# Indirect writes of a routed layer in two bursts, and its first loads ahead of the inverse copies

## The chip, the cores and the metric

The kernel runs on one core of a Trainium2 chip. The metric is the device time of one execution in microseconds. Engines are TensorE (PE), VectorE (DVE), ScalarE (ACT), GpSimd (POOL) and the DMA queues that SyncE, ScalarE and GpSimd feed.

## The reference, cut to what matters

Four layers work on x (8 sequences of 256 rows, 256 columns) and on a context of the same shape, all in float32, each adding to x:

```
x = x + mlstm_attention(layernorm(x), ctx, ctx)             # layer 1
x = x + moe32(layernorm(x))                                 # layer 2
x = x + fft_convolution_and_two_ffns(ctx, layernorm(x))     # layer 3
x = x + dense_moe8(x)                                       # layer 4

# layer 2, moe32: 2048 tokens, top 4 of 32 experts, H = 128
weights, indices = top_k(softmax(xf @ Wg), 4)
for e in range(32):
    tok = tokens that chose e (at most 1024)
    y[tok] += (silu(xf[tok] @ W1[e]) * (xf[tok] @ W3[e])) @ W2[e] * weight
out = y + silu(xf @ Ws1) * (xf @ Ws3) @ Ws2                 # shared expert

# layer 3, the part computed beside layer 2: a long convolution of the context
zn = layernorm(ctx @ W_in + b_in) * g + beta
dcw = irfft(rfft(filter) * rfft(zn))                        # first rows, per sequence
```

## The kernel before, in words

All engines run their own instruction streams and meet in semaphores. After the attention the stretch that matters has four strands, which overlap.

**Shared expert and context rows.** TensorE computes the shared expert of layer 2 in eight steps; VectorE multiplies (line 663), rounds (the cast of line 668) and forms the low part (line 810, `hL`) of each step, since every float32 product is made of a high and a low part. Between these steps VectorE takes statistics of the context rows `zn`, ScalarE normalises them (line 1325, semaphore `z_normed`), and gain and shift are put on: for quarters 0 and 1 by VectorE (lines 803 and 804, behind steps 6 and 7), for quarters 2 and 3 by POOL (`affine(2)` and `affine(3)`, lines 1660 and 1661, two passes over 128 x 1024 each).

**Routing writes on POOL.** Each of the 2048 tokens goes into four slots of a buffer in HBM, `slots_in`, ordered by expert. POOL does it with 64 indirect writes (`scatter`, line 1642), each of one row per partition, 128 rows of 1 KB, whose places come from `idS`. All signal one semaphore, `scattered`, and behind every fourth POOL waits until all writes so far have landed. The order on POOL is written out by hand: 32 writes, affine(2), 8 writes, affine(3), 24 writes, then `split_expert(e)` for the 32 experts: two passes over 128 x 768 each (line 1633 copies the high part of the weights from stage `eS` into the ring `eHL` of six, line 1635 makes the low part). In front of expert 3 POOL waits for the last product of the transform (`prod_dve` 6) and the last spectrum, because the ring slots of experts 3 to 5 lie on the buffers of the spectra. Experts 0 to 2 have no such wait.

**The transform.** It goes in six blocks, n = 0 to 5. TensorE makes a spectrum (line 1969), ScalarE copies it (line 1336, `Zs`), VectorE multiplies it with the filter's spectrum in seven instructions (lines 836, 837, 839 to 843), each waiting for the one before, and TensorE transforms back (line 1985). Line 839 must wait for the inverse of the block before, since it overwrites `PR`; lines 836 and 837 need not. `PI`, written by line 843, releases the inverse. The order on TensorE is spectrum 0, spectrum 1, then spectrum n + 2 and inverse n in turns; in front of the last inverse stand 32 spare matmuls (line 1719), which compute nothing that is used. Blocks 2 and 5 work on two quarters of the rows each. ScalarE copies the results out of PSUM into `dcw` (`inverse_copy`, line 1330): copies 0 and 1 between spectrum copies, copies 2 and 3 behind the last inverse.

**The routed tiles.** 48 pairs of tiles of 128 slots. ScalarE gives out the loads (`load_pair`, line 1361, a ring of four) and rounds; TensorE transposes a pair (line 2008), waiting at first for all eight inverse copies (`inv_copied` 8), multiplies it with its expert's weights (`tile_up`, line 2028, waiting for `ew_ready`), transposes and multiplies again (lines 2037 and 2047); VectorE forms low parts (line 850). The stores go to `slots_out`, from which POOL later gathers (line 1687). After them come the feed-forward blocks of layer 3 and the 32 expert blocks of layer 4 (lines 1921 and 1937).

## Time and profile before

| | us |
|---|---|
| median of 3 runs | 1806.13 (1804.2 to 1808.56) |
| span of the profiled execution | 1787.3 |
| median less that span | 18.8 |
| TensorE busy | 1667.1 (93%) |
| VectorE busy | 1207.9 (68%) |
| ScalarE busy | 474.6 (27%) |
| POOL busy | 471.5 (26%) |
| mean granted TensorE clock, share of full | 0.971 |

The span runs from the first to the last instruction of one execution; the device time of that same execution is not listed apart from the three runs, so it stands beside their median. Times below count from the span's start. In a timeline a row is: start, duration, engine, line, operation, written and read tensors, and in brackets the idle time before it and what ended it. ACTq is ScalarE's issuing of DMAs. TensorE's full clock is 2.4 GHz, its lower level 1.2 GHz (0.50). The writes of line 1648 lie between 213.3 and 350.8, the transform between 268 and 349, the routed tiles between 354 and 513.

### The profile page before, as it was taken

How to read it: one execution, taken by the hardware profiler on the slowest of the kernel's cores; microseconds unless marked ns; L12 is line 12 of the kernel's file. 1: busy time of each engine (PE TensorE's matmuls, PEld its weight loads, DVE VectorE, ACT ScalarE, POOL GpSimd, SP SyncE). 2: the span in 40 equal slices, each digit the busy share in tenths (PEclk: the TensorE clock that was granted, in tenths of full speed). 3: DMA queues.
4: the chain of work that ended last, by engine and by line, in shares of the span. 5: the costliest groups of instructions: out<-in, count | busy, mean ns of one | idle time of the engine just before them, and what ended most of it. 6: DMA issues, size and time to landing. Idle time of an engine off the chain costs nothing.

```text
span 1787.3 us, 29133 instructions
## 1 busy us (share of the span) xinstructions
PE 1667.1 (93%) x9784; PEld 1439.4 (81%) x9785; DVE 1207.9 (68%) x2483; ACT 474.6 (27%) x836; POOL 471.5 (26%) x355
## 2 busy tenths in 40 slices
PE   6998987799956898999999999999999999999998
PEld 5997673388854787888888888888888888888887
DVE  6457777556656895666666766766766766766765
ACT  3445322134432464211211211211111111111111
POOL 4274257688426601100100100100100100100100
PEclk9998999899978998999999999999999999999999
DMA  9200022278643200000000000000000000000001
GB/s 368 91 1 30 16 73 96 89 250 272 200 127 119 72 1 19 19 36 18 19 34 18 20 33 18 21 32 18 21 32 18 23 30 18 26 27 18 18 0 48
DMA packets 53827, 106.53 MB, mean 60 GB/s; under 512 B 6528, under 2 KB 37696, under 8 KB 53632
## 3 DMA queue, kind: packets, MB, share of 16 engines
q1 hardware_dynamic: 19920, 63.33, 10.4%
q10 hardware_dynamic: 27696, 25.51, 4.5%
q0 software_dynamic: 6144, 16.79, 2.9%
q8 instruction: 43, 0.70, 0.2%
q14 instruction: 24, 0.20, 0.0%
HBM read 69.96 MB, written 35.65 MB: 59 GB/s over the span
## 4 chain that ended last, share of the span: by engine, by line
PE 80%; DVE 6%; issue 4%; POOL 4%; DMA 4%; ACT 2%; SPq 0%; POOLq 0%; DVEq 0%; another core or an unknown queue 0%; ACTq 0%
PE ps L1921 39%; PE ps L1937 20%; PE ps L2028 4%; DMA slots_in<-xn,idS 2%; POOL slots_in L1648 2%; PE ps L2047 2%; PE ps L1772 2%; PE ps L2103 1%; PE ps L2125 1%; PE ps L2008 1%; DVE x L917 1%; DMA x<-in_x 1%; PE ps L1773 1%; PE ps L1789 1%; PE ps L1790 1%
## 5 line engine op out<-in xcount | busy, mean ns | idle before, releaser
L1921 PE MATMUL ps<-xTH,wH 128*128 128x512 f32 x1024 | 402.5, 393 | 2.1 <-DVE hF L1161 2.1
L1921 PE MATMUL ps<-xTH,wL 128*128 128x512 f32 x1024 | 402.2, 393 | 0.0
L1921 PE MATMUL ps<-xTL,wH 128*128 128x512 f32 x1024 | 398.9, 390 | 0.0
L1309 ACT ACTIVATE sg<-ps 128x512 f32<-128x512 f32 x264 | 157.9, 599 | 885.3 <-PE ps L1921 885.3
L1161 DVE TENSOR_TENSOR hF<-sg,ps 128x512 f32<-128x512 f32 x256 | 175.7, 686 | 302.1 <-ACT sg L1309 302.1
L1620 POOL TENSOR_TENSOR wL<-wS,wH 128x1536 fp32r<-128x1536 f32 x32 | 111.9, 3496 | 959.8 <-ACT wH L1304 959.8
L1937 PE MATMUL ps<-wL,hH 128*128 128x256 f32 x1024 | 289.8, 283 | 0.0
L1937 PE MATMUL ps<-wH,hL 128*128 128x256 f32 x1024 | 289.7, 283 | 0.0
L1937 PE MATMUL ps<-wH,hH 128*128 128x256 f32 x1024 | 288.6, 282 | 0.5 <-DVE hL L1170 0.5
L1170 DVE TENSOR_TENSOR hL<-hF,hH 128x512 fp32r<-128x512 f32 x256 | 258.0, 1008 | 0.1
L1921 PEld LDWEIGHTS ps<-xTL,wH 128*128 128x128 f32 x1024 | 192.8, 188 | 42.2
L1180 DVE SCALAR_TENSOR_TENSOR x<-ps,cw,x 128x256 f32<-128x256 f32 x512 | 222.6, 476 | 1.0 <-PE ps L1937 1.0
L1921 PEld LDWEIGHTS ps<-xTH,wH 128*128 128x128 f32 x1024 | 193.6, 189 | 36.1 <-ACT sg L1309 1.9
L1921 PEld LDWEIGHTS ps<-xTH,wL 128*128 128x128 f32 x1024 | 193.8, 189 | 30.5
L1937 PEld LDWEIGHTS ps<-wH,hH 128*128 128x128 f32 x1024 | 195.5, 191 | 10.6 <-DVE hL L1170 0.7
L1937 PEld LDWEIGHTS ps<-wH,hL 128*128 128x128 f32 x1024 | 195.5, 191 | 9.8
L1937 PEld LDWEIGHTS ps<-wL,hH 128*128 128x128 f32 x1024 | 195.5, 191 | 0.0
L1164 DVE CAST hH<-hF 128x512 fp32r<-128x512 f32 x256 | 109.3, 427 | 38.8 <-PE ps L1937 30.2
L1648 POOL DMA_INDIRECT slots_in<-xn,idS x64 | 76.6, 1197 | 59.6 <-DMA slots_in<-xn,idS 29.7
L2028 PE MATMUL ps<-eHL,hH 128*128 x384 | 81.5, 295 | 2.2 <-POOL eHL L1635 2.2
L1687 POOL DMA_INDIRECT yg<-slots_out,idG x48 | 50.0, 1041 | 69.2 <-DMA slots_out<-yo 49.0
L603 DVE SCALAR_TENSOR_TENSOR Cm<-ps,Dm 128x384 f32<-128x384 f32 x64 | 35.6, 557 | 47.1 <-ACT Dm L1272 43.0
(385 smaller groups left out, 2525.4 us busy)
## 6 DMA issues: line engine op xcount, KB each, us to landing
wS<-in_w SPq DMA_DIRECT2D x32, 768.0 KB, 4.3
slots_in<-eS SPq DMA_DIRECT2D x16, 768.0 KB, 20.2
eS<-in_wr SPq DMA_DIRECT2D x32, 384.0 KB, 3.9
xl<-slots_in ACTq DMA_DIRECT2D x48, 256.0 KB, 3.9
slots_out<-yo ACTq DMA_DIRECT2D x48, 256.0 KB, 3.1
cx<-in_ctx SPq DMA_DIRECT2D x1, 2048.0 KB, 10.4
x<-in_x SPq DMA_DIRECT2D x2, 1024.0 KB, 13.8
out<-x SPq DMA_DIRECT2D x4, 512.0 KB, 2.9
```

Of the source, the lines that this page charges most:

```text
L1161: dve.tensor_tensor(hF[:, b, :], sg[:, b, :], ps[:, 2 + b, :], ALU.mult).then_inc(mul_done, 1)
L1164: dve.tensor_copy(hH[:, b, :], hF[:, b, :]).then_inc(h_high, 1)
L1170: dve.tensor_tensor(hL[:, b, :], hF[:, b, :], f32(hH[:, b, :]), ALU.subtract).then_inc(h_low, 1)
L1180: dve.scalar_tensor_tensor(x[:, tile, :], acc, cw2[:, tile, bass.ds(it, 1)], x[:, tile, :], ALU.mult, ALU.add).then_inc(evac_done, 1)
L1309: act.activation(sg[:, b, :], ps[:, b, :], ACT.Silu).then_inc(silu_done, 1)
L1620: pool.tensor_tensor(blocks(wL, slot, plain), blocks(wS, slot, plain), f32(blocks(wH, slot, plain)), ALU.subtract).then_inc(w_low, 1)
L1648: pool.indirect_dma_start(xs_d, bass.IndirectOffsetOnAxis(ap=idS[:, n, k:k + 1], axis=0), xn[:, n, :], None, bounds_check=TILES * P - 1, o ...
L1687: pool.indirect_dma_start(slot_rows(n)[:, k, :], None, ys_d, bass.IndirectOffsetOnAxis(ap=idG[:, n, k:k + 1], axis=0), bounds_check=TILES ...
L1772: pe.matmul(ps[:, i % 2, 0:256], kT[:, c, t0:t0 + P], qM[:, i % 12, :], start=True, stop=True)
L1921: last = pe.matmul(ps[:, 2 * half + b, :], piece(w, s, slot, col, P), v[:, k, g * 512:(g + 1) * 512], start=q == 0, stop=q == 5)
L1937: last = pe.matmul(o, h[:, b, t * P:(t + 1) * P], piece(w, s, slot, col, D), start=(opens and t % 2 == 0 and q == 0), stop=(closes and q = ...
L2028: last = pe.matmul(ps[:, 2 + b, t * D:(t + 1) * D], h[:, b, (2 * t + k) * P:(2 * t + k + 1) * P], eFlat[:, bass.ds(off + (w + k * D), D)], ...
```

## The change

Three edits:

- POOL's writes signal two semaphores in turns, one burst of four on the one, the next on the other. Behind each burst from the second on POOL waits for the landing of the burst before, no longer for its own. Behind the last write it waits for the last burst.
- ScalarE waits for both semaphores in place of the one.
- On ScalarE that wait, three more that stood with it, and the first four `load_pair` are moved in front of `inverse_copy(2)`, `inverse_copy(3)` and the wait for the last product.

```diff
-        scattered = sem("scattered")
+        scattered = [sem("scattered_even"), sem("scattered_odd")]
@@ scalar
             spectrum_copy(5)
-            inverse_copy(2)
-            inverse_copy(3)
-            act.wait_ge(prod_dve, 6)
...
-            act.wait_ge(scattered, 64 * 16)
+            for burst in scattered:
+                act.wait_ge(burst, 64 * 8)
             act.wait_ge(evac_done, 4 * M_FA)
             wait_low(act, 8)
             act.wait_ge(table_done, 1)
             for q in range(4):
                 load_pair(q, q)
+            inverse_copy(2)
+            inverse_copy(3)
+            act.wait_ge(prod_dve, 6)
             for q in range(2):
                 tile_high(q, q)
                 load_pair(q + 4, q)
@@ gpsimd, scatter
-                                            bounds_check=TILES * P - 1, oob_is_err=False).then_inc(scattered, 16)
+                                            bounds_check=TILES * P - 1, oob_is_err=False).then_inc(scattered[sent[0] // 4 % 2], 16)
                     sent[0] += 1
-                    if sent[0] % 4 == 0:
-                        pool.wait_ge(scattered, 16 * sent[0])
+                    if sent[0] % 4 == 0 and sent[0] > 4:
+                        before = sent[0] // 4 - 2
+                        pool.wait_ge(scattered[before % 2], 64 * (before // 2 + 1))
@@ gpsimd
             scatter(NT * TOPK - 40)
+            pool.wait_ge(scattered[1], 64 * 8)
             pool.wait_ge(table_done, 1)
```

## Rows read from the trace of the kernel before

**Rows 1.** The page's chain that ended last, by line.

```profile
PE ps L1921 39%; PE ps L1937 20%; PE ps L2028 4%; DMA slots_in<-xn,idS 2%; POOL slots_in L1648 2%; PE ps L2047 2%; PE ps L1772 2%; PE ps L2103 1%; PE ps L2125 1%; PE ps L2008 1%; DVE x L917 1%; DMA x<-in_x 1%; PE ps L1773 1%; PE ps L1789 1%; PE ps L1790 1%
```

**Rows 2.** The chain of waits, 340 to 380: start, us, what.

```profile
358.04 2.92 PE ps L2028 x12
363.62 1.43 PE ps L2028 x12
```

**Rows 3.** POOL's timeline, 348 to 358: start, us, instruction, idle before.

```profile
348.38 0.97 POOL L1648 DMA_INDIRECT slots_in<-xn,idS  x1 [0.30 <-issue]
350.88 1.46 POOL L1633 TENSOR_TENSOR eHL<-eS,zcol 128x768 fp32r<-128x768 f32 x1 [1.52 <-DMA slots_in<-xn,idS]
355.72 1.81 POOL L1635 TENSOR_TENSOR eHL<-eS,eHL 128x768 fp32r<-128x768 f32 x1
```

**Rows 4.** Timelines of ScalarE, TensorE and VectorE, 349 to 357.

```profile
349.03 2.06 ACT L1330 ACTIVATE dcw<-ps 128x512 f32<-128x512 f32 x4 [24.12 <-PE ps L1985]
350.87 1.96 ACTq L1361 DMA_DIRECT2D xl<-slots_in  x4
353.87 1.94 PE L2008 MATMUL ps<-ident,xl 128*128 128x128 f32 x8 [4.88 <-DMA xl<-slots_in]
355.69 1.48 DVE L850 TENSOR_TENSOR hL<-ps,hH 128x512 fp32r<-128x512 f32 x2 [12.28 <-ACT hH L1370]
```

**Rows 5.** Line 1648: durations min/median/max in ns, and POOL's idle time before it.

```profile
L1648 POOL DMA_INDIRECT slots_in<-xn,idS x64: 967/976/3037, 213.3 to 348.4; - x64
  DMA slots_in<-xn,idS: 29.7, 13
```

**Rows 6.** Timelines around the shared experts: ScalarE, VectorE and TensorE, 253 to 266.

```profile
253.53 2.07 ACT L1325 ACTIVATE zn<-zn,sd,rs 128x256 f32<-128x256 f32 x4
259.08 0.69 DVE L810 TENSOR_TENSOR hL<-hF,hH 128x512 fp32r<-128x512 f32 x1
265.33 0.51 PE L1937 MATMUL ps<-sH,hH 128*128 128x256 f32 x1 [2.62 <-DVE hL L810]
```

**Rows 7.** POOL's groups, 299.9 to 350.5: busy, mean ns, idle before.

```profile
L1648 POOL DMA_INDIRECT slots_in<-xn,idS x24 | 32.8, 1366 | 17.4 <-DMA slots_in<-xn,idS 11.2 <-issue 5.5 <-POOL zn L1661 0.8
```

**Rows 8.** Timelines of POOL and VectorE where both compute, 274 to 300.

```profile
293.51 2.35 POOL L1660 TENSOR_TENSOR zn<-zn,bcv 128x1024 f32<-128x1024 f32 x1 [1.52 <-DMA slots_in<-xn,idS]
295.94 3.20 POOL L1661 TENSOR_TENSOR zn<-zn,bcv 128x1024 f32<-128x1024 f32 x1
274.04 4.35 DVE L836 TENSOR_TENSOR tv<-Zs,WG 128x2048 f32<-128x2048 f32 x1 [4.39 <-ACT Zs L1336]
293.70 3.25 DVE L842 TENSOR_TENSOR tv<-tv 128x1024 f32<-128x1024 f32 x1
296.98 2.71 DVE L843 TENSOR_TENSOR PI<-tv 128x512 f32<-128x512 f32 x1
```

**Rows 9.** Timelines of VectorE and POOL, 310 to 314.

```profile
310.45 2.29 DVE L836 TENSOR_TENSOR tv<-Zs,WG 128x2048 f32<-128x2048 f32 x1
310.77 2.81 POOL L1648 DMA_INDIRECT slots_in<-xn,idS  x1 [0.30 <-issue]
```

**Rows 10.** VectorE's timeline, end of the first product.

```profile
284.18 0.69 DVE L843 TENSOR_TENSOR PI<-tv 128x512 f32<-128x512 f32 x1
```

**Rows 11.** VectorE's groups, 271.3 to 350.

```profile
L840 DVE TENSOR_TENSOR tv<-Zs,WG 128x1024 f32<-128x1024 f32 x6 | 7.4, 1226 | 0.2
L839 DVE TENSOR_TENSOR PR<-tv 128x512 f32<-128x512 f32 x6 | 4.2, 692 | 10.3 <-PE ps L1985 10.3
```

**Rows 12.** Line 1985 by stretch: window, length, busy (x), granted clock, DMA, GB/s.

```profile
286.70:290.30 3.60, 3.55 (x8) 1.33 (x7) 1.00 0.20 72
299.70:305.00 5.30, 5.25 (x8) 2.08 (x8) 0.69 0.10 36
331.70:338.10 6.40, 6.33 (x8) 2.41 (x8) 0.58 0.13 44
```

**Rows 13.** POOL's timeline after sixteen gathers.

```profile
545.21 1.12 POOL L1687 DMA_INDIRECT ya<-slots_out,idG  x1 [4.80 <-DMA yg<-slots_out,idG]
```

## The prediction

> **What bounds the kernel now.** I read the page's chain first: TensorE's matmuls carry it, and lines 1921 and 1937 alone, the experts of the last layer, are 59% [rows 1]. The change touches none of that. It touches the 75 us ahead of the routed tiles, where the chain runs over POOL's indirect writes. I therefore read the end of that stretch. The first product of the tiles (line 2028) starts at 358.04 [rows 2]. Two branches lead to it. On POOL the last write is issued at 348.38, its landing is awaited, and four passes of 1.46 to 1.82 us split experts 0 and 1 by 357.53 [rows 3]. On the other side the inverse transform ends on TensorE at 349.0, ScalarE makes four copies, only then gives out the first pair loads at 350.87, and TensorE waits 4.88 us for the data until 353.87; VectorE has the first low part at 355.69 + 0.74 = 356.4 [rows 4]. POOL is the last of the two, by 1.1 us (the product starts 0.5 us behind its release), and the loads are right behind. I call the end of the inverse transform X: X = 349.0, and the tiles start at X + 9.05.
>
> **The bursts.** POOL waits 29.7 us in 13 places for a landing [rows 5]. With two bursts out, the older burst has 4 x 1.28 us to land, against 2.5 us from the last issue to its landing (348.38 to 350.88), so I take every such wait as gone; an issue gap of 0.30 stays: 29.7 - 3.9 = 25.8 us. The first 32 writes then take 32 x 1.28 = 41 us from 213.3 and, I allow, 1.5 more for collisions: the first affine on POOL starts at about 256, 15 us sooner (seven waits of 2.0 net, and a landing of 1.5), just when its input is ready (253.53 + 2.07) [rows 6]. Its two passes take 4.7, then 8 writes some 12.5 with their collisions: the second affine starts near 273.5 in place of 293.5. The 24 writes left had a mean of 1.37 us [rows 7] and a gap of 0.30: 40 us from 279, the end near 319, and with the landing the first expert pass near 320 in place of 350.9.
>
> **What that sets free, and what it collides with.** POOL is then no longer the last branch. But experts 0 to 2 are not held back by the products (only expert 3 is), so their six passes, 3 x (1.47 + 1.82) = 9.9 us, move from behind the products into them. The trace says what two such instructions do to each other. POOL's pass at 293.51 ended at 295.86; VectorE's pass begun at 293.70 took 3.25 us, and ended 1.1 us after POOL's; POOL's next pass then took 3.20 against the first one's 2.35, and VectorE's next one 2.71. The first product's multiply at 274.04 took 4.35, too [rows 8]. Undisturbed, such passes of VectorE take 2.29, 0.69 and 1.23 us [rows 9 to 11]. Each waits for the other's end, in turns. In the same way an indirect write begun at 310.77 ended 0.84 us after the multiply begun at 310.45. The Trainium skill (SBUF — State Buffer, Who interferes with whom) states that a VectorE instruction with two SBUF inputs and a GpSimd one that reads SBUF exclude each other, the second waiting in full. That speaks against this change, and the rows agree; the sum below goes by the rows.
>
> Step by step, against X:
>
> 1. The first affine moves to 256 to 261, into the shared experts. VectorE's low part at 259.08 has two SBUF inputs and will wait for POOL's second pass. VectorE sets the end of this stage: TensorE waits for its last low part until 265.33 [rows 6]. I take +2.0 us. Bounds: 0 if it fits between, and 4.7 if both passes lie on VectorE's way. The cast of line 668 has one input, and no row shows it beside a POOL pass, so I leave it at nothing. By the skill's same section a cast may take the shared ports as well; by that the step would be nearer its upper end.
> 2. The second affine lands on the first product, in place of the first affine there (+2.06 before, about the same now). That product has cover: its last multiply ended at 284.87 and the first inverse, behind a spectrum on TensorE, began only at 286.7 [rows 10, 12]. Cost 0; if both passes hit, 2.3 more against 1.9 of cover, so up to 0.4.
> 3. The second product loses its collision: -(3.25 - 1.23) - (2.71 - 0.69) = -4.05 us. TensorE then idles 4 us less before the second inverse. That inverse ran at a granted clock of 0.69, half speed for part of it, and took 5.3 us; the first one, right behind a spectrum, ran at 1.00 and took 3.6 [rows 12]. I take -1.65, with 0 as the other end.
> 4. The six expert passes start near 320, in the fifth product. The products run in a ring: the inverse on TensorE, then lines 839 to 843 on VectorE (0.69 + 3 x 1.23 + 0.69, 5.2 with gaps) [rows 11], then the next inverse. Lines 836 and 837 of the next product lie beside the inverse, with a mean slack of 10.3 / 5 = 2.1 us before line 839. So one or two passes hide there and four or five alternate with lines 839 to 843, each costing its length less 0.13. I went through it with the first pass at 320, 322, 324 and 328 and got 6.5, 5.5, 5.3 and 6.0. I take +6.2. Ends: 0 if these passes do not hold VectorE, and 9.9 if all of them are on its way.
> 5. The fifth inverse already starts cold (0.58, 6.4 us) [rows 12]. Before it TensorE will now idle 6 us longer; I keep its price, with 6.4 x 0.58 / 0.50 = 7.4, so +1.0, as the upper end. The 32 spare matmuls still lie under the last product.
>
> X moves by 2.0 - 4.05 - 1.65 + 6.2 = +2.5, to 351.5.
>
> 6. Behind X: ahead of the copies ScalarE is idle for 24 us, from the last spectrum copy on [rows 4]; the writes have landed near 320, so the four loads' 1.96 us of issue falls into that idle time, and the data are there long before X. The wait on the writes stands in front of two inverse copies, whose input comes 30 us after the writes; it holds nothing. TensorE then transposes right behind the copies: X + 2.2 in place of X + 4.9. From there to the first product the old path took 356.4 - 353.87 = 2.6 us. X + 4.8 in place of X + 9.05, with experts 0 and 1 long split: -4.25. Experts 3 to 5 may start with the last product, 5 us ahead of X, so no tile waits for them. The first 12 matmuls of the tiles ran in 2.92 us, later ones in 1.43 [rows 2]; if the shorter idle time keeps the clock up, another -1.5. I take -0.3 of it.
>
> Sum: +2.5 - 4.25 - 0.3 = -2.0 us. The tiles are a chain on TensorE, and all behind them is dependent, so this passes to the end. The profiled execution's span is 1787.3 us; the runs' median is 1806.1, so 18.8 us lie around the span, and I leave them as they are: 1804.1 us. About 0.2% (3.6 us) is what a measurement of this kernel can tell from no change.
>
> **Rivals.**
> A, the collisions cost little. Only affine passes of 1024 columns are seen to hold a product; beside the expert passes VectorE so far ran instructions with a PSUM input alone. If step 4 is 0 to 1, the sum is -2.0 - 5.7 = -7.7: 1798.4. Against it: line 1635 reads two tensors just as the affine does. 0.27.
> B, slower: POOL keeps the ports from one pass to the next. Its passes follow one another within 0.08 us; it gave way to VectorE in the one pair that I can see [rows 8]. If it does not in this place, step 4 costs 9.9 (+3.7), the fifth inverse stays cold throughout (+1.0) and steps 1 and 2 go to their ends (+2.7 + 0.4): -2.0 + 7.8 = +5.8, 1811.9. It decides from 5.6 us above my sum. 0.12.
> C, the writes pile up, so POOL is done no sooner. For: after bursts of 16 indirect gathers POOL waited 4.80 us for the last landing, not 1.5 [rows 13]. Against: those gathers were themselves issued without a stall. The loads would then still be issued before the copies, and 2 us of issue would be given back: -1 to +1, 1806. 0.09.
>
> **The numbers.** My forecast has 0.52: 1804.1, its own range 1800.5 to 1807.5 (steps 1, 3 and 6 at their nearer ends); 0.06 of it reaches below -3.6 us and 0.01 above +3.6. Faster: 0.27 + 0.06 = 0.33. Slower: 0.12 + 0.01 = 0.13. Same: 0.54. The range 1797.5 to 1808.5 takes in A and leaves out most of B.
>
> **What would show it.** Right: no wait of POOL for a landing between bursts; the last write issued near 318; experts 0 to 2 split between 320 and 335, and in that stretch four or five of VectorE's multiplies at 2.3 to 3 us; lines 842 and 843 of the second product back at 1.23 and 0.69; inverse end near 351.5; the first tile product about 5 us behind it. Wrong: multiplies of 1.23 beside the expert passes and X near 345 (A); expert passes back to back with a multiply of 4 us or more beside them (B); writes of more than 2 us with no multiply beside them (C).

## The result, and the profile after

The change made the kernel slower: 1830.9 us (median of 5, 1829.7 to 1838.3) against 1804.2 us (1799.1 to 1808.6) on the same chip, a ratio of 1.0169 (95% interval 1.0145 to 1.0192). That is 27 us between the medians and 30 us by the ratio. The forecast was 1804.1 with a range of 1797.5 to 1808.5.

POOL did what was foreseen. The first and the last of the first 32 writes, then the first pass of the first affine (POOL's timeline of the changed kernel):

```profile
211.51 1.39 POOL L1649 DMA_INDIRECT slots_in<-xn,idS  x1 [13.63 <-issue]
...
251.92 0.97 POOL L1649 DMA_INDIRECT slots_in<-xn,idS  x1 [0.30 <-issue]
277.08 2.39 POOL L1662 TENSOR_TENSOR zn<-zn,bcv 128x1024 f32<-128x1024 f32 x1 [24.19 <-ACT zn L1325]
```

Between 211.51 and 251.92 the writes follow one another at 1.28 us, without a wait. But where POOL was to go on at 256, as `z_normed` was signalled at 255.6 before [rows 6], it waits 24.19 us for it, until 277.08. The reason lies in the other engines, in the same 40 us. VectorE and ScalarE (timelines of the changed kernel):

```profile
253.66 0.34 DVE L763 COPY etf<-ps 1x192 f32<-1x192 f32 x1 [27.33 <-remote]
...
257.45 0.60 ACT L1309 ACTIVATE sg<-ps 128x512 f32<-128x512 f32 x1 [27.14 <-remote]
```

TensorE (timeline, 228 to 260):

```profile
228.40 0.49 PE L1952 MATMUL ps<-ident,tc 96*1 96x96 f32 x4
...
231.04 0.40 PE L1924 MATMUL ps<-xTH,sH 128*128 128x512 f32 x1
231.27 0.40 PE L1924 MATMUL ps<-xTH,sL 128*128 128x512 f32 x1
...
232.55 0.40 PE L1924 MATMUL ps<-xTH,sH 128*128 128x512 f32 x1 [0.22 <-issue]
233.96 0.39 PE L1924 MATMUL ps<-xTH,sL 128*128 128x512 f32 x1 [1.01 <-issue]
234.68 0.48 PE L1924 MATMUL ps<-xTM,sH 128*128 128x512 f32 x1 [0.34 <-issue]
236.09 0.40 PE L1924 MATMUL ps<-xTH,sH 128*128 128x512 f32 x1 [0.94 <-issue]
...
258.59 0.58 PE L1940 MATMUL ps<-sH,hH 128*128 128x256 f32 x1 [19.88 <-DVE hL L810]
```

VectorE's line 763 needs only the small transposes of 228.40, over at 228.9. It starts at 253.66, 25 us later; ScalarE's line 1309 needs a product that TensorE had done at 238.7 and starts at 257.45, 19 us later. "remote" is the name for a wait whose end no recorded signal explains. Both end behind the last write (251.92 + 0.97). In the kernel before, the same line 763 started 0.04 us behind the end of its transposes (230.71):

```profile
230.75 0.35 DVE L763 COPY etf<-ps 1x192 f32<-1x192 f32 x1 [2.60 <-PE ps L1949]
```

TensorE slows down as well before it stops: from 232.55 on its matmuls start 1.41, 0.72 and 1.41 us apart instead of 0.23 (231.04 to 231.27), with idle time put down to "issue". So three engines stand still while POOL's writes stream: VectorE and ScalarE for 27 us, TensorE for 20, the last of it waiting for VectorE. The windows say the same. Columns: stretch, length, busy time and instructions of PE, PEld, DVE, ACT and POOL, clock, DMA share, GB/s. The changed kernel:

```profile
213.00:253.00 40.00, 21.33 (x91) 14.28 (x91) 9.45 (x27) 4.87 (x7) 30.55 (x31) 0.80 0.28 102
```

The same stretch of the kernel before:

```profile
213.00:253.00 40.00, 36.34 (x173) 28.10 (x174) 31.54 (x104) 10.69 (x19) 23.18 (x23) 0.96 0.20 72
```

VectorE is busy for 9.45 us instead of 31.54, TensorE for 21.33 instead of 36.34. The DMA engines are busy 0.28 of the time, so they are not full. And in the changed kernel's chain of waits (start, us, what) the piece is this:

```profile
226.32 27.31 another core or an unknown queue
```

The expert passes then hit the transform, as foreseen, though in the fourth product and not in the fifth (changed kernel, POOL, then VectorE):

```profile
340.25 1.46 POOL L1634 TENSOR_TENSOR eHL<-eS,zcol 128x768 fp32r<-128x768 f32 x1 [1.59 <-issue]
341.79 2.13 POOL L1636 TENSOR_TENSOR eHL<-eS,eHL 128x768 fp32r<-128x768 f32 x1
343.88 2.45 POOL L1634 TENSOR_TENSOR eHL<-eS,zcol 128x768 fp32r<-128x768 f32 x1
...
329.62 1.22 DVE L842 TENSOR_TENSOR tv<-tv 128x1024 f32<-128x1024 f32 x1
...
340.63 1.63 DVE L839 TENSOR_TENSOR PR<-tv 128x512 f32<-128x512 f32 x1 [5.40 <-PE ps L1988]
342.29 2.71 DVE L840 TENSOR_TENSOR tv<-Zs,WG 128x1024 f32<-128x1024 f32 x1
345.03 2.37 DVE L841 TENSOR_TENSOR tv<-Zs,WG 128x1024 f32<-128x1024 f32 x1
347.44 2.71 DVE L842 TENSOR_TENSOR tv<-tv 128x1024 f32<-128x1024 f32 x1
350.18 1.84 DVE L843 TENSOR_TENSOR PI<-tv 128x512 f32<-128x512 f32 x1
```

One more loss lies just ahead of that product, and no step of the prediction has it: the wait of 5.40 us of line 839, against 2.03 in the kernel before. The third inverse took 8.9 us (331.6 to 340.5, granted clock 0.62) where before it took 5.5 (310.4 to 315.9, granted clock 1.00). TensorE had idled 1.9 us ahead of it in both, so what brought the clock down is not shown. Four of its matmuls, changed kernel and kernel before:

```profile
334.34 2.08 PE L1988 MATMUL ps<-PR,GI 64*128 64x512 f32 x4
...
312.22 1.13 PE L1985 MATMUL ps<-PR,GI 64*128 64x512 f32 x4
```

And the end of the transform, the loads and the first tile (ScalarE, TensorE, VectorE; answers to [rows 2, 4]):

```profile
352.29 1.96 ACTq L1358 DMA_DIRECT2D xl<-slots_in  x4
379.33 2.06 ACT L1330 ACTIVATE dcw<-ps 128x512 f32<-128x512 f32 x4 [25.34 <-PE ps L1988]
...
381.50 1.06 PE L2011 MATMUL ps<-ident,xl 128*128 128x128 f32 x8 [2.20 <-issue]
384.83 0.58 PE L2031 MATMUL ps<-eHL,hH 128*128 x1 [2.27 <-DVE hL L850]
...
382.92 1.29 DVE L850 TENSOR_TENSOR hL<-ps,hH 128x512 fp32r<-128x512 f32 x2 [9.20 <-ACT hH L1367]
```

The loads are given out at 352.29, 27 us ahead of the copies; X is 379.3 and the tiles start at X + 5.5, where before it was X + 9.05 [rows 2, 4].

Executions reach this stretch at different times, so from here on I measure from one mark that stands ahead of all that changes: the start of TensorE's last `ps<-ident,tc` transposes (228.40 after, 230.22 before, 227.5 to 236.1 in the other kernels). From the mark to the first tile's product it is 127.8 us before and 156.4 us after, +28.6. The input of POOL's first affine comes 23 us later (48.5 against 25.4), and the first product ends 24.9 us later. The second inverse then comes another 3.8 us later (the spectrum ahead of it took 8.80 us against 7.1). The second product, free of its collision, gives 4.1 back and its inverse 1.5. The third inverse adds 3.4, the expert passes 6.2, the rest is -0.5, and the path behind X gives 3.55 back. That is the 30 us of the ratio, to within what a measurement tells. A single profile tells such sums to some 3 us only: two other kernels (of the gathers, below) have the code of the kernel before up to the tiles, and there it is 130.5 and 127.7 us. The two profiled spans differ by more, 46.1 us, for two reasons that have nothing to do with the change: the profiled execution after took 1835.2 us for a span of 1833.4, so only 1.8 us lie around a span, and that of before was therefore a 1789 us one, below all of its timed runs; and among the gathers the changed kernel's has waits "remote" that before's has not (below).

### The profile page after: what moved, and what is told of

Its sections match the earlier page's. It is cut to its first block, busy times and chain, and to the rows that moved or that the text cites. A ratio compares the mean times of both kernels' runs of the same rounds, so it can differ in the third digit from the quotient of the medians.

```text
span 1833.4 us, 29134 instructions
## 1 busy us (share of the span) xinstructions
PE 1678.4 (92%) x9784; PEld 1446.4 (79%) x9785; DVE 1213.8 (66%) x2483; ACT 474.7 (26%) x836; POOL 470.7 (26%) x355
## 4 chain that ended last, share of the span: by engine, by line
PE 81%; DVE 9%; issue 4%; ACT 2%; another core or an unknown queue 2%; DMA 1%; SPq 0%; DVEq 0%; ACTq 0%
PE ps L1924 39%; PE ps L1940 20%; PE ps L2031 4%; PE ps L2050 2%; PE ps L1775 2%; PE ps L1988 2%; PE ps L2106 1%; PE ps L2128 1%; PE ps L2011 1%; PE ps L1972 1%; DMA x<-in_x 1%; DVE x L917 1%; PE ps L1776 1%; PE ps L1792 1%
## 5 line engine op out<-in xcount | busy, mean ns | idle before, releaser
L1649 POOL DMA_INDIRECT slots_in<-xn,idS x64 | 73.1, 1142 | 33.8 <-issue 29.2
```

The source lines that it names most:

```text
L1649: pool.indirect_dma_start(xs_d, bass.IndirectOffsetOnAxis(ap=idS[:, n, k:k + 1], axis=0), xn[:, n, :], None, bounds_check=TILES * P - 1, o ...
```

## The experiments

The name "the standstill" is used for the waits above. Theory S: a stream of indirect writes without a gap causes it, and it is the whole loss. Rivals: L, the hoisted loads do it; K, the collisions with the expert passes.

**The bursts alone, and the loads alone.** The first has the new waits of POOL with ScalarE's order of before; the second has ScalarE's new order with the waits of before.

> The two bursts alone; the loads stay behind the last inverse copies. Theory S (stream): 32 indirect writes given out by POOL with no pause for 41 us hold back the signals that TensorE sends, so VectorE stands still for some 27 us until the last of them is out. Then this kernel has the same standstill (VectorE line 763 starts within 1 us of the end of the 32 writes, 25 to 28 us late) and the whole loss: 1828 to 1835 us. Rival L (the hoisted loads or the wait in front of the copies cause the loss): 1800 to 1806 and no standstill. Rival K (collisions of VectorE's multiplies with POOL's passes of experts 0 to 2 cause it): 1806 to 1812, no standstill, multiplies of 2.3 us and more.

> The hoisted loads alone, on the kernel before; one burst in flight. Theory S: no standstill, and POOL is still the last branch at the first tile, so 0 to +2 us against the kernel before: the four loads' 2 us of issue now lies in front of the last copies when the writes land only at 350.8. Rival L: 20 us or more slower. Rival K: as S.

The bursts alone gave 1827.8 against 1800.9, ratio 1.0157 (1.0133 to 1.0180); the loads alone 1801.8, ratio 1.0004 (0.9990 to 1.0018). L falls. S was met in the time and for ScalarE, but only in part for VectorE. Its line 763 was expected 25 to 28 us late, at the end of the writes; it started at 243.16, 12.7 us late and 11 us ahead of that end. The bursts alone have the standstill all the same (waits of that kernel, 210 to 300: who, for what, sum, times, longest):

```profile
ACT sg L1309 <- remote: 29.2, 1, 29.2
...
DVE etf L763 <- remote: 15.2, 1, 15.2
```

The loads alone gain nothing for a reason of their own: without the bursts the writes land near 351, ScalarE waits for them in front of inverse copies 2 and 3, and the copies come at 353.43, though the inverse was over at 345.8. The tiles start 130.8 us behind the mark. ScalarE's timeline of the loads-alone kernel:

```profile
351.44 1.95 ACTq L1358 DMA_DIRECT2D xl<-slots_in  x4
353.43 2.06 ACT L1330 ACTIVATE dcw<-ps 128x512 f32<-128x512 f32 x4 [30.75 <-issue]
```

**A gap after every fourth write.** The changed kernel with linked memsets of one column; eight of them, then two:

```diff
+                    if sent[0] % 4 == 0:
+                        for _ in range(8):      # in the second kernel: 2
+                            link(pool.memset(zcol[:, :], 0.0))
```

> The changed kernel, and POOL sets one column of zeros eight times, in a chain, behind every fourth write: a pause of about 2 us that waits for no landing. Theory S: the stream has holes again, the standstill of VectorE at line 763 is gone or under 3 us, and the time is 1798 to 1808. Rival F (what matters is how many writes are in flight, not the lack of a pause): by the time of the pause all but the last write have landed in both, so this rival can only say that the landing wait itself matters: standstill kept, 1825 to 1835. Rival K: 1806 to 1812.

> The changed kernel with two linked memsets of one column (about 0.3 us of work, a gap of some 1.2 us between writes instead of 0.30) after every fourth write; eight of them gave a gap of about 2.4 us and no standstill. At a landing of about 2.4 us after the issue, with a gap of 1.2 us the queue of writes is never empty. Theory P (a gap on POOL is what lets the others' signals through, however short): no wait 'remote' over 2 us, VectorE's L763 starts before 235, time 1800 to 1806. Rival Q (the queue of writes must run empty once): the standstill is there as in the changed kernel, L763 starts after 250, time 1820 to 1832. In between: a standstill of part of the length.

No standstill in either. Ratios 1.0006 (0.9987 to 1.0025) and 1.0026 (1.0008 to 1.0044): the loss of 1.7% is gone or nearly so. The second needs only this (its timeline, POOL and then VectorE):

```profile
229.72 0.28 POOL L1657 MEMSET zcol<- 128x1 f32 x2
230.80 0.97 POOL L1649 DMA_INDIRECT slots_in<-xn,idS  x1 [0.80 <-POOL zcol L1657]
...
229.66 0.35 DVE L763 COPY etf<-ps 1x192 f32<-1x192 f32 x1 [2.60 <-PE ps L1955]
```

The write before the memsets ended at 229.73, so the gap is 1.07 us. At 2.4 us from issue to landing, the median of this kernel's writes, the queue doesn't run empty in it, so that is not the condition. The kernel with eight memsets ran on the chip of the bursts alone, which has the standstill; that of two ran on another, but its gap in the first 32 writes was enough too on a chip where longer pieces have the standstill ("The best of both", below). S stands.

**Pacing the first 32 writes, with and without the collisions.** In the first of these kernels POOL waits for a burst's own landing in the first 32 writes and is two bursts deep behind them. The second also moves the wait for the sixth product in front of expert 0, so that all expert passes come behind the products. The third is the second with the four loads back behind the copies.

```diff
-                        before = sent[0] // 4 - 2
+                        before = sent[0] // 4 - (1 if sent[0] <= 32 else 2)
...
-                if e == 3:
+                if e == 0:
                     pool.wait_ge(prod_dve, 6)
```

> The changed kernel, but for the first 32 writes POOL waits for each burst's own landing as before; two bursts are in flight only in the last 32. Theory S: the long gapless stretch is gone from the shared experts; the later stretches of 8 and 24 writes lie beside the transform, where TensorE's signals are needed at every product. If any gapless stretch stalls, there is a standstill of up to 25 us there; in the changed kernel's trace none is seen beside the 24 writes, so I expect none: 1796 to 1806. Rival K: the expert passes collide with the multiplies as in the changed kernel (8 to 9 us in one product): 1806 to 1812.

> The version with the first 32 writes in paced bursts (wait for a burst's own landing) and the last 32 two bursts deep, with all of POOL's expert passes held until the sixth product is done (the wait for prod_dve stands before expert 0, not before expert 3). Theory K (the six expert passes and VectorE's products of 339 to 354 us hold each other up): the products L836 to L843 take 1.2 to 1.6 us again, L843 of the sixth ends about 350 in place of 356.7, the first tile's product starts near 366 in place of 372, and the time comes down from 1810 to about 1803. Rival C (TensorE's inverses at the low clock are what ends last there, the collisions are hidden beside them): L843 of the sixth ends within 2 us of 356.7 and the time stays at 1808 to 1812. Rival E (the experts are then late for the first expert tiles): the products are early but the first expert tile waits for POOL's L1636, time 1808 or more.

> The version with paced first bursts and late experts, but with the four pair loads back behind the last copies of the inverse transform, as in the kernel before. Step 6 of the prediction (with POOL done early, hoisting the loads takes 4.25 us off the way from the last copy to the first tile): the first tile's product starts 3 to 5 us later than in the run with the hoist (357.1 there, with 1788.4 us span) and the ratio to before is 0.002 higher than with it (0.999). Rival (the loads' landing is hidden behind the transposes' own work): the first tile's product within 1 us of it, the same ratio.

First: ratio 1.0050 (1.0029 to 1.0070), no standstill, 139.1 us from the mark to the tiles. Second: 0.9990 (0.9974 to 1.0005), 128.6 us. The passes beside the products thus cost some 10.5 us, as the ratios say too (0.6%). The first five instructions of the last product, with the passes beside them (VectorE, first kernel):

```profile
341.27 3.70 DVE L836 TENSOR_TENSOR tv<-Zs,WG 128x2048 f32<-128x2048 f32 x1
345.01 2.37 DVE L837 TENSOR_TENSOR tv<-tv 128x1024 f32<-128x1024 f32 x1
347.81 1.79 DVE L839 TENSOR_TENSOR PR<-tv 128x512 f32<-128x512 f32 x1 [0.43 <-PE ps L1988]
349.63 2.37 DVE L840 TENSOR_TENSOR tv<-Zs,WG 128x1024 f32<-128x1024 f32 x1
352.03 2.71 DVE L841 TENSOR_TENSOR tv<-Zs,WG 128x1024 f32<-128x1024 f32 x1
```

And without them (second kernel):

```profile
335.28 2.29 DVE L836 TENSOR_TENSOR tv<-Zs,WG 128x2048 f32<-128x2048 f32 x1
337.61 1.22 DVE L837 TENSOR_TENSOR tv<-tv 128x1024 f32<-128x1024 f32 x1
340.74 0.69 DVE L839 TENSOR_TENSOR PR<-tv 128x512 f32<-128x512 f32 x1 [1.90 <-PE ps L1988]
341.46 1.22 DVE L840 TENSOR_TENSOR tv<-Zs,WG 128x1024 f32<-128x1024 f32 x1
342.72 1.22 DVE L841 TENSOR_TENSOR tv<-Zs,WG 128x1024 f32<-128x1024 f32 x1
```

The five take 12.94 us with the passes beside them and 6.64 without, 6.3 less. The rest comes behind them: the last inverse took 9.0 us (356.7 to 365.7) after the slow products and 5.6 (345.9 to 351.5) after the quick ones. Its matmuls ran at half pace in most of it (2.08 us for four, against 1.13). K is true and worth 10 us, give or take the 3 us by which single profiles differ. The second kernel is as fast as the one before, no faster than it can be told. Third: ratio 1.0001 (0.9981 to 1.0021). From the first inverse copy to the first tile it takes 7.33 us (347.58 to 354.91) against 5.50 (351.55 to 357.05) with the loads hoisted. So with POOL early hoisting is worth 1.8 us here, half of what its expectation said, and less than a ratio can show. In the other kernels with the loads hoisted that path takes 5.5 us in some and 6.4 in others, so it is 1 to 1.9 us.

**How long may the stream be.** Four kernels change only where the first 32 writes are interrupted: a wait for the own landing behind writes 8, 16, 24 and 32; a gap of 1.1 us (two memsets) behind write 16 alone; behind write 24 alone; behind 8, 16 and 24.

```diff
-                        before = sent[0] // 4 - 2
+                        before = sent[0] // 4 - (1 if sent[0] in (8, 16, 24, 32) else 2)
```

```diff
+                    if sent[0] in (8, 16, 24):    # or == 16, or == 24
+                        for _ in range(2):
+                            link(pool.memset(zcol[:, :], 0.0))
```

> The changed kernel, but after writes 8, 16, 24 and 32 POOL waits until the burst it has just sent has landed (after the others one burst stays in flight). So the writes stream without a pause for 8 x 1.28 = 10.2 us and stand still for about 2.5 us. Theory S1 (signals are held only while the stream runs and get through at every pause): VectorE's L763 waits at most 10 us instead of 27, each hand-over between engines there loses up to one stretch of 10 us, and the time lies at 1803 to 1815. Rival S2 (it takes more than 10 us of unbroken stream before anything is held): no wait 'remote' over 2 us in 210 to 260 us, time 1799 to 1806. Rival S3 (what matters is the number of writes in flight at all, not the pauses): the 27 us standstill as before, 1828 to 1832.

> The changed kernel with one pause only (two linked memsets, a gap of 1.10 us) after write 16 of the first 32, so two unbroken stretches of 16 writes, 20 us each. In the changed kernel the other engines stopped about 18 us into the stretch (VectorE's L763 due at 230). Theory O (it takes a stretch of some 18 us before signals are held, and any gap starts the count again): the second stretch ends just before its hold would bite, no wait 'remote' over 3 us, time 1.000 to 1.003 of before. Rival A (a signal that is sent anywhere in an unbroken stretch is held to its end): waits 'remote' up to 20 us that end at the pause (near 232) and at the end of the second stretch (near 253), ratio 1.008 to 1.015.

> The changed kernel with one pause only, after write 24 (near 242 us), so an unbroken stretch of 24 writes, 31 us, and one of 8. Theory (the standstill ends with the unbroken stretch, whatever the other engines do meanwhile): VectorE's L763, due at 230, starts at 242 to 244 instead of 253.7, the wait 'remote' there is 13 to 16 us instead of 27.3, and the ratio to before is 1.006 to 1.012 instead of 1.017. Rival (the standstill lasts until all of the writes are through, or until a refill of instructions that comes at 259 in the changed kernel): L763 at 253 or later, ratio 1.015 to 1.019.

> The changed kernel with a gap of 1.1 us after writes 8, 16 and 24. Theory B (TensorE's signals are served more slowly than they are sent while the writes stream, a backlog builds up, and a gap serves a part of it; one gap was too little, seven were enough): with three gaps the waits 'remote' are between those, VectorE's L763 (due at 230) starts between 231 and 239 and ScalarE's L1309 waits 3 to 20 us instead of 27 to 29; ratio 1.003 to 1.012. Rival H (signals are held until the unbroken stretch ends): then each gap frees what was sent before it, nothing waits 'remote' for more than 10 us, ratio 1.002 to 1.005. Rival T (what counts is that a stretch stays under some 10 writes): no wait 'remote' over 2 us, ratio 1.001 to 1.003.

| interruption of the first 32 | median of before on that chip | longest unbroken | VectorE's wait at 763 | ScalarE's at 1309 | mark to tiles | ratio (interval) |
|---|---|---|---|---|---|---|
| none (the change) | 1804.2 | 32 | 27.3 | 27.1 | 156.4 | 1.0169 (1.0145 to 1.0192) |
| none, loads not hoisted | 1800.9 | 32 | 15.2 | 29.2 | 156.6 | 1.0157 (1.0133 to 1.0180) |
| gap after 24 | 1801.4 | 24 | 13.8 | 29.1 | 153.0 | 1.0136 (1.0100 to 1.0171) |
| gap after 16 | 1801.4 | 16 | 9.6 | 29.1 | 152.6 | 1.0125 (1.0094 to 1.0156) |
| gap after 8, 16, 24 | 1792.2 | 8 | 2.3 | 6.2 | 132.3 | 1.0000 (0.9984 to 1.0017) |
| landing after 8, 16, 24, 32 | 1792.7 | 8 | 2.4 | 6.2 | 134.9 | 1.0035 (1.0014 to 1.0056) |
| gap after each 4, in all 64 | 1792.7 | 4 | 2.6 | 6.2 | 136.1 | 1.0026 (1.0008 to 1.0044) |
| gap of 2.0 us after each 4, in all 64 | 1800.9 | 4 | 2.6 | 6.2 | 135.9 | 1.0006 (0.9987 to 1.0025) |
| landing after each 4 | 1800.9 | 4 | 2.6 | 6.2 | 139.1 | 1.0050 (1.0029 to 1.0070) |
| gap after each 4, experts late (below) | 1801.4 | 4 | 2.6 | 6.2 | 125.7 | 0.9990 (0.9970 to 1.0010) |
| kernel before: landing after each 4 | 1804.2 | 4 | 2.6 | 6.2 | 127.8 | 1 |

(About 2.6 and 6.2 us are what these two instructions wait in the kernel before, too.) Two more expectations fell. One gap behind write 16 was to cure all or to end the waits in front of it, and did neither. With the gap behind 24, line 763 should have started at 242 to 244; it started at 239.59, 2.6 us ahead of the gap, so a gap is not what lets it go, and the ratio was outside what was expected. ScalarE's wait was 29.1 us in both, to 3.4 us behind the last write. The kernel with the gap behind 24 (timeline; POOL, VectorE, ScalarE):

```profile
242.20 0.28 POOL L1657 MEMSET zcol<- 128x1 f32 x2
...
252.21 0.97 POOL L1649 DMA_INDIRECT slots_in<-xn,idS  x1 [0.31 <-issue]
...
239.59 0.34 DVE L763 COPY etf<-ps 1x192 f32<-1x192 f32 x1 [13.78 <-remote]
...
256.63 0.60 ACT L1309 ACTIVATE sg<-ps 128x512 f32<-128x512 f32 x1 [29.12 <-remote]
```

So signals are not simply held until a stream ends. They come late: there line 763's signal (its transposes ended at 228.4) came 11 us late, ScalarE's (its product ended at 233.0) 24 us. With three gaps nothing comes late at all, which rival T alone had said; with the landings of 8, S2 had.

What is shown: 16, 24 or 32 writes in one piece did harm, and 4 in one piece, with a gap or a landing behind them, did none on the same chips (medians of before of 1800.9 and 1801.4 us). The two rows with pieces of 8 prove less than they seem to. They were taken on the two other chips (1792.2 and 1792.7), where no profile of any kernel has a wait "remote", not even beside gathers that go out 16 in a piece, and where neither the change nor pieces of 16 or 24 writes ever ran. So that 8 writes (10 us) in one piece do no harm, as T and S2 have it, is not shown: it may have been the chip. A backlog that builds up in a long stretch and goes off in a gap when it is small fits the rows; that it was too large to go off in the one gap is argued, not shown.

**The gathers.** Behind the routed tiles POOL gathers in pieces of 16. The kernel before with a wait for the landing every 8 gathers, and with the 1.1 us gap (two memsets) behind every 4:

```diff
-                if n in (4, 8, 12):
+                if n in (2, 4, 6, 8, 10, 12, 14):
                     pool.wait_ge(gathered[(n - 1) % YG], ((n - 1) // YG + 1) * TOPK * 16)
```

> The kernel before, with POOL waiting for the landing of its gathers after every 8 (n = 2, 4, 6 ...) instead of after every 16. Theory G (the gathers' stream of 16 without a pause, too, makes the other engines stand still in some executions, and this is the 15 us by which the profiled execution of before lies under its median): each of the four added waits costs POOL about 2.5 us, 10 us in all, of which part is hidden, but no wait 'remote' over 2 us is left in 560 to 660 us and the runs lie closer together; time 1790 to 1800. Rival N (the gathers' stand-still is not of this kind, or doesn't reach the end): the four waits only add, 1801 to 1812.

> The kernel before, with two linked memsets (a gap of 1.1 us) after every fourth gather; the gathers otherwise run in unbroken stretches of 16, 20 us. Theory G (in some executions the gathers' stretches hold TensorE's signals up as the writes' do, waits 'remote' of 7 to 13 us near 610 to 650, and this is most of the spread of the runs of before; the waits for landings of the earlier run cost what they saved): the 16 gaps cost at most 0.8 us each on POOL, 12.8 us, partly beside the waits for VectorE; no wait 'remote' over 2 us in 540 to 660, a spread of the runs under 8 us and a ratio of 0.996 to 1.000. Rival N (the spread is of another kind): the same spread as before and a ratio of 1.000 to 1.006.

The reason for these was a row such as this, of the loads-alone kernel (waits, 540 to 720):

```profile
ACT xTH L1431 <- remote: 8.7, 2, 7.9
```

Ratios 1.0018 (1.0004 to 1.0032) and 1.0026 (1.0013 to 1.0040): the interruptions only cost, 3 and 5 us. But they were no test. Waits "remote" of 6 to 13 us among the gathers stand in all eight profiles taken on two of the chips, whose medians of before were 1800.9 and 1801.4 us, and in none of the eight taken on two others, at 1792.7 and 1792.2 us, whatever the kernel. These two kernels ran where there was nothing to remove. The profile of before doesn't fit a rule by chips, though: it has no such wait, at 1789 us against a median of 1804. What decides it stays open.

**The best of both.** The gap of 1.1 us after each fourth of the first 32 writes, all expert passes behind the products, loads hoisted; then the same with the gap every 4 and every 8 gathers. Its edits are those shown, with `sent[0] % 4 == 0 and sent[0] <= 32` for the gap.

> The changed kernel with two linked memsets after each fourth of the first 32 writes (the gap of 1.10 us that was enough), none after that, and POOL's expert passes held until the sixth product is done. If the two losses found (the standstill; the expert passes beside the products) are all there is against the change, the sixth product ends near 341 us on a chip where it ended at 349.8 with the passes beside it, the first tile's product starts at 352 to 354 against 358 to 359 in the kernel before, and the ratio to before is 0.995 to 0.998. Rival: TensorE's inverses at the low clock set the products' pace whatever POOL does; then the sixth product ends at 345 or later, the first tile's product is no earlier than 357 and the ratio is 0.999 to 1.001.

> The version with gaps in the first 32 writes and late experts (0.999 so far, its first tile's product 2.1 us earlier than in the kernel before, but with a wait 'remote' of 13.4 us among the gathers), with the gap after every fourth gather as well. If theory G holds: no wait 'remote' over 2 us anywhere, ratio 0.993 to 0.998. Rival N: 0.998 to 1.004.

> The same with a gap after every eighth gather only (8 gaps, at most 6.4 us of POOL's time). If a gap of 1.1 us per 8 is enough to let the backlog go: ratio 0.2 to 0.3% below the version with 16 gaps. If it is not: waits 'remote' of 5 to 13 us among the gathers again and a ratio at or above that version's.

The first has the tiles 125.7 us behind the mark, 2.1 less than before, where 5 were expected, and a ratio of 0.9990 (0.9970 to 1.0010). The others have them at 128.6 and 128.5, with ratios of 1.0004 (0.9986 to 1.0021) and 0.9995 (0.9980 to 1.0010). None of them can be told from the kernel before, and these two, too, ran where the gathers had nothing to remove. In the last one the products wait for TensorE's inverses (VectorE, fourth and fifth product):

```profile
319.11 0.76 DVE L839 TENSOR_TENSOR PR<-tv 128x512 f32<-128x512 f32 x1 [3.70 <-PE ps L1994]
...
329.61 0.69 DVE L839 TENSOR_TENSOR PR<-tv 128x512 f32<-128x512 f32 x1 [1.59 <-PE ps L1994]
```

With POOL out of the way TensorE's spectra and inverses set the pace (3.70 us of waiting here, 1.59 in the next block). That was the rival in the first of these expectations. It was met in the ratio and nearly in the end of the sixth product (344.9, where it said 345 or later and the theory 341), but not in the first tile's product (355.96, where it said 357 or later). What POOL's being early is worth here, 2.1 us in one profile, is within the 3 us by which single profiles differ.

## Why the prediction was wrong

What failed is one step, in the part on the bursts: "the first affine on POOL starts at about 256 ... just when its input is ready (253.53 + 2.07)". I moved POOL's own work and let every other engine keep its times of before. POOL's side was right to about a microsecond (32 writes in 41.4 us where I had 42.5, the last at 251.92, no landing waited for). But TensorE, VectorE and ScalarE, which share nothing with the writes that I had costed, stood still, and the input came at 277 (line 763 alone waited 27.33 us, and the first product ended 24.9 us later against the mark). I had treated the waits that the change removes as pure loss. They were also the pauses in which the others' signals got through, and none of my three rivals had a price for their absence; my upper bounds summed to +5.8 us, and the miss was 27 (1830.9 against 1804.1). Nothing in the profile of before shows it: its longest stretch of writes is 4. The gathers of before, 16 in a piece [rows 13], were the nearest row; I used them for how long a landing takes. What the other engines did beside them would not have warned me in that profile, which has no wait "remote" there; the waits of 6 to 13 us stand in profiles of the two chips named above.

By its steps:

- **Waits gone (25.8 us): right.** The idle gap of 0.30 us is all that is left. Rival C (writes pile up) is refuted.
- **Step 1: a little too small, step 2: right.** The kernel with three gaps, where the first affine lies at 254.6 to 259.5 as foreseen, shows step 1 by itself. The low part of line 810 took 2.75 us beside the second pass instead of 0.69, which is the +2.0. The cast of line 668, which I had left at nothing, took 1.14 instead of 0.43 beside the first pass. The first spectrum is copied 3.2 us later from the mark (45.0 against 41.8), and the first product's multiply took 3.95 us against 4.35. VectorE in that kernel:

```profile
256.16 1.14 DVE L668 CAST hH<-hF 128x512 fp32r<-128x512 f32 x1
257.33 2.75 DVE L810 TENSOR_TENSOR hL<-hF,hH 128x512 fp32r<-128x512 f32 x1
```

- **Step 3: right for the product, uncertain for the clock.** The second product is free of collisions (lines 840 to 842 from 318.05 to 321.8 take 1.23, 1.23 and 1.22 us in the changed kernel) and gives 4.1 us back where I had 4.05. Its inverse gave 1.5 of my 1.65 back in the changed kernel and nothing in the kernel with three gaps (5.4 us against 5.3).
- **Step 4: right in kind and size.** I had +6.2 us from four or five passes in turns. In the changed kernel they fell into the fourth product: 1.63, 2.71, 2.37, 2.71, 1.84 in place of 0.69, 1.23, 1.23, 1.23, 0.69 is 6.2 us. With the passes and without them five instructions of the last product differed by 6.3. Rival A is refuted, and rival B too: POOL and VectorE took turns. The Trainium skill's rule (SBUF — State Buffer, Who interferes with whom) that two such instructions exclude each other agrees with these rows, for passes of 768 columns as for those of 1024.
- **Step 5: the wrong inverse.** The fifth inverse, which I had priced, was no slower: 5.6 us in the changed kernel against 6.4. But the third took 8.9 us instead of 5.5 there and in six of the kernels without the standstill, +3.4 that stand in none of my steps. And in three of those (a gap after each 4 in both sizes, and the paced one) the last inverse took 8.9 to 9.0 us instead of 5.6, most of it at half pace. TensorE had idled 3.89 us ahead of it in the paced kernel and 0.16 us in the one with late experts; I had counted on the 32 spare matmuls to lie there.
- **Step 6: right in kind, 3.55 us of 4.25.** POOL being early gives 1.7 (9.05 to 7.33), the hoisting 1.8 (1 to 1.9 over all kernels). The first 12 matmuls of the tiles took 2.92 us as before, so the 0.3 was not there.
- **The sum without the standstill.** In the kernel with three gaps X is 8.0 us later than before (126.8 against 118.8 from the mark) and the tiles 4.5 us later, where I had +2.5 and -2.0. Against the mark the 8.0 come as 3.2 from step 1, -3.9 from step 3, 3.3 from the third inverse (8.9 us at a granted clock of 0.62) and 5.4 from the expert passes and what followed them; its last inverse took 5.6 us as before. With the experts late X is at 119.2 to 123.1 from the mark in five kernels, and the third inverse is slow in two of them, in part in one. But a kernel whose code is that of before up to there has X at 122.0 in its profile, where before has 118.8, so these differences are not the change's for certain. The ratio of the kernel with three gaps, 1.0000 (0.9984 to 1.0017), has my forecast in its interval. With the tiles 6.5 us later in its profile than my steps have them, that agreement would have been partly luck.
- **Around the span.** I put 18.8 us around the span; it is 1.8. The profiled execution of before was 15 us quicker than the median, most likely by the waits among the gathers that it did not have.

## What to carry to other kernels

A wait behind each few indirect DMAs may be doing something for the other engines. Before it is removed, replace it by a short gap (here 1.1 us after every 4), and look whether other engines wait for signals that were sent long before; compare the time of a small instruction on VectorE with its producer's end. And work that is moved out from behind a chain must not be let into it: POOL's passes with two SBUF operands, moved beside VectorE's products, cost some 10 us, of which 3.4 came from the lower clock of the engine that had waited.

## What was not expected of the hardware

A stream of 16 or more indirect writes of 128 KB, 1.28 us apart with 0.30 us between them, made signals from TensorE arrive 7 to 25 us late and made TensorE itself issue at steps of 0.72 and 1.41 us, at a DMA share of 0.28; with the bursts alone and with the gap after 24 TensorE's steps were of 2.1 us as well (250.17, 252.24, 254.35, 256.44 in the former). Pieces of 4 with a gap of 1.1 us between them did not, on the same chips. Pieces of 8 were tried only on chips where nothing of the kind was ever seen, not even beside gathers 16 in a piece, and what sets these chips apart is open. The last 24 writes of the changed kernel (299.6 to 337.7) run without a gap as well and show nothing of the kind; there VectorE's multiplies hold single writes for up to 2.8 us, which may act as gaps: at most nine go out 1.28 us apart (311.54 to 321.74). That was not tried.

What is late is open: the signals, TensorE's supply of instructions, or the recording. In the changed kernel no packet of instructions arrives between 205 and 258.8, where before two came at 241 and one at 254; with a gap after 24 one came at 245. Both came 0.2 to 0.6 us behind the matmul with which TensorE goes on (258.59 and 244.52), so they may be an effect of its standing still and not the cause. The Trainium skill (NOTIFIC — the notification-queue block, section 7.1 on overflow) says that the block which writes an engine's profile records holds its producers back rather than lose a record inside itself, and that this can throttle an engine. Every execution timed here lists a span, so each was recorded in some form, and no run shows what an unrecorded one would do. If that rule is behind it, part or all of the 30 us belongs to the measurement. The comparison would have to be repeated without a profiler before the change is given up for it; what would be left by the kernel with three gaps is no gain either.
